# Gathers of a mixture-of-experts stage: four tiles a step for eight, and each gather waits for the last one

## What is computed

```python
edge_index = jnp.stack([src, dst])
x = x + _L0_gnn_ref(_layernorm(x), weight, bias, edge_index, edge_type_8)
x = x + _L0_ffn_ref(_layernorm(x)[None], gate_w, gate_b, w1, w2, w3)[0]

# _L0_gnn_ref: messages of 53125 edges of 8 types, summed over each target node
h_all = jnp.einsum('ni,roi->rno', node_repr, weight)
messages = jax.ops.segment_sum(h_all[edge_types, src], dst, num_segments=node_repr.shape[0])

# _L0_ffn_ref: the two best of 16 experts for each node, weighted
top_probs, top_idx = jax.lax.top_k(jax.nn.softmax(x @ gate_w + gate_b), 2)
hidden = jax.nn.silu(x @ w1[e]) * (x @ w2[e])      # hidden size 512
out = sum over the two experts of prob[e] * (hidden @ w3[e])
```

## Time and profile before

| | us |
|---|---|
| median of 3 runs | 969.27 |
| lowest, highest | 967.42, 971.19 |
| span of the profiled execution | 1205.6 |
| PE busy in it | 802.0 (67%) |
| POOL busy in it | 655.2 (54%) |
| DVE busy in it | 517.7 (43%) |
| mean granted clock of TensorE | 0.83 |

### The profile page before, as it was taken

How to read it: one execution, slowest core, us unless ns; L and a number is a source line. 1 busy time by engine, 2 the same in 40 slices (tenths; PEclk the granted TensorE clock), 3 DMA queues, 4 the chain that set the end, 5 groups by cost and what they waited for, 6 DMA issues and landing times.

```text
span 1205.6 us, 18175 instructions
## 1 busy us (share of the span) xinstructions
PE 802.0 (67%) x4527; PEld 664.8 (55%) x4528; DVE 517.7 (43%) x1480; ACT 262.8 (22%) x390; POOL 655.2 (54%) x614
## 2 busy tenths in 40 slices
PE   1355566666666677574666668657898889887761
PEld 1233355555555555463555556546787678776650
DVE  6753333333434344334333336786343334332327
ACT  5501111111111221111111111411232223221213
POOL 1366555555555666566555554045648583876442
PEclk9976687878878887797787788869898889997885
DMA  9434333333333322232222322336446554553325
GB/s 231 122 91 120 105 102 111 107 110 105 104 104 104 106 85 83 78 108 83 74 75 78 99 74 67 127 102 203 142 153 201 170 171 157 166 169 92 95 83 151
DMA packets 91426, 141.83 MB, mean 118 GB/s; under 512 B 13143, under 2 KB 65835, under 8 KB 91402
## 3 DMA queue, kind: packets, MB, share of 16 engines
q0 software_dynamic: 25680, 70.16, 20.2%
q1 hardware_dynamic: 48800, 56.26, 14.7%
q10 hardware_dynamic: 16922, 15.15, 3.9%
HBM read 108.59 MB, written 32.93 MB: 117 GB/s over the span
## 4 chain that ended last, share of the span: by engine, by line
PE 41%; another core or an unknown queue 18%; issue 17%; DVE 11%; DMA 4%; DVEq 4%; ACT 3%; ACTq 1%; SPq 1%; POOL 1%; POOLq 0%
PE ps L1426 16%; PE ps L1565 9%; PE ps L1547 6%; PE ps L1414 5%; DVE hot L981 2%; PE ps L1573 2%; PE ps L1456 2%; DVE store L999 2%; DMA acc<-in_x 1%; ACT store L699 1%; DVEq L999 1%; DVE stat L1016 1%; DVE ps L1348 1%; DVE acc L1012 1%
## 5 line engine op out<-in xcount | busy, mean ns | idle before, releaser
L541 POOL DMA_INDIRECT got<-x_tab,idx x425 | 403.5, 949 | 338.7 <-DVE idx L1001 188.6
L1414 PE MATMUL ps<-hot,got 125*128 125x256 f16 x1700 | 220.3, 289 | 65.3 <-issue 40.9
L999 DVE TENSOR_TENSOR store<-store,ps 128x512 f32 x150 | 103.0, 687 | 335.3 <-PE ps L1414 156.4
L1414 PEld LDWEIGHTS ps<-hot,got 125*128 125x128 f16 x1700 | 173.2, 103 | 110.8 <-issue 77.6
L1426 PE MATMUL ps<-part,store 128*128 128x256 f32 x800 | 222.4, 444 | 8.9 <-issue 8.4
L1426 PEld LDWEIGHTS ps<-part,store 128*128 128x128 f32 x800 | 180.1, 229 | 42.0 <-issue 11.3
L1565 PE MATMUL ps<-part,operands 128*128 x696 | 191.0, 426 | 6.9 <-DVE operands L1277 4.1
L1565 PEld LDWEIGHTS ps<-part,operands 128*128 128x128 f32 x696 | 137.6, 205 | 38.2 <-issue 8.8
L981 DVE TENSOR_SCALAR hot<-key_row,pass,drel 125x256 f16<-125x256 f16 x425 | 126.4, 354 | 74.0 <-issue 73.8
L1456 PE MATMUL ps<-gw_sb,x2T 128*125 128x16 f32 x100 | 23.1, 349 | 172.8 <-ACT x2T L691 105.2
L1547 PE MATMUL ps<-part,operands 128*128 x696 | 104.5, 303 | 30.8 <-DVE operands L1287 30.8
(11 more groups left out here) (229 smaller groups left out, 637.6 us busy)
## 6 DMA issues: line engine op xcount, KB each, us to landing
store<-in_L_ffn_w SPq DMA_DIRECT2D x48, 512.0 KB
y_tab<-ffn SPq DMA_DIRECT2D x9, 896.0 KB
y_tab<-ffn ACTq DMA_DIRECT2D x58, 128.0 KB
xs_tab<-x_sb SPq DMA_DIRECT2D x14, 512.0 KB
ffn<-xs_tab ACTq DMA_DIRECT2D x55, 128.0 KB
got<-x_tab,idx POOLq DMA_INDIRECT x425
acc<-in_x SPq DMA_DIRECT2D x5, 560.0 KB
x_tab<-got SPq DMA_DIRECT2D x5, 560.0 KB
```

The source lines that it names most:

```text
L541: nc.gpsimd.indirect_dma_start(got[:, c, :], None, x_tab, bass.IndirectOffsetOnAxis(ap=idx[:, c:c + 1], axis=0)).then_inc(gathered[c], 16)
L999: v.tensor_tensor(window, window, ps[:, WIN_BANK[g], :].rearrange("p (q n) -> p q n", n=WIN), ALU.add).then_inc(win_added, 1)
L1414: last = mm(ps[:, WIN_BANK[g], k * KEYS:(k + 1) * KEYS], got[0:CE, c, a * DIM + k * P:a * DIM + (k + 1) * P], hot[0:CE, g % HOT, c - c0, : ...
```

## The change

OCT, 8 tiles to a step, becomes QUAD, 4 tiles, and with it the half step that SP stores becomes two tiles (256 KB) for four. DVE's table quad_end counts in steps of four. The second part: inside a step, each gather from the second on waits until the one before has landed, and the 25 gathers of the first results do so too. The second results' gathers are as before.

```diff
-OCT = 8
-HALF_OCT = OCT // 2
+QUAD = 4
+HALF_QUAD = QUAD // 2
...
-                    sp.wait_ge(oct_got[n], (q + 1) * HALF_OCT * 16)
+                    sp.wait_ge(quad_got[n], (q + 1) * HALF_QUAD * 16)
...
-            def gather_oct(q):
+            def gather_quad(q):
                 pool.wait_ge(xs_stored, (q * 2 + 1) * 16)
                 pool.sem_inc(slot_free, 1)
-                nc.gpsimd.tensor_copy(oct_idx[:, :], token[:, bass.ds(q * OCT + DIRECT, OCT)]).then_inc(oct_ready, 1)
-                pool.wait_ge(oct_ready, q + 1)
+                nc.gpsimd.tensor_copy(quad_idx[:, :], token[:, bass.ds(q * QUAD + DIRECT, QUAD)]).then_inc(quad_ready, 1)
+                pool.wait_ge(quad_ready, q + 1)
                 pool.sem_inc(slot_free, 1)
-                for u in range(OCT):
+                for u in range(QUAD):
+                    if u:
+                        n = u - 1
+                        pool.wait_ge(quad_got[n // HALF_QUAD], q * HALF_QUAD * 16 + (n % HALF_QUAD + 1) * 16)
+                        pool.sem_inc(slot_free, 1)
                     nc.gpsimd.indirect_dma_start(
...
             for t in range(TILES):
                 if t % LOAD == 0:
                     wait_stored(0, t + LOAD - 1)
+                if t:
+                    pool.wait_ge(y_got[t - 1], 16)
                 nc.gpsimd.indirect_dma_start(
                     y1[:, t, :], None, y_tab,
                     bass.IndirectOffsetOnAxis(ap=pos2[:, 0, t:t + 1], axis=0)).then_inc(y_got[t], 16)
...
-                act.wait_ge(xs_stored, (j // HALF_OCT + 1) * 16)
+                act.wait_ge(xs_stored, (j // HALF_QUAD + 2 - DIRECT // HALF_QUAD) * 16)
```

More of the change, by code:

```diff
@@ L77 @@
 DIRECT = 4
-OCT = 8
-HALF_OCT = OCT // 2
-OCTS = -(-(SLOT_TILES + 2 - DIRECT) // OCT)
-XS_TILES = OCTS * OCT
+QUAD = 4
+HALF_QUAD = QUAD // 2
+QUADS = -(-(SLOT_TILES + 2 - DIRECT) // QUAD)
+XS_TILES = QUADS * QUAD
 ZT = 7
@@ L241, in build @@
         xs_ahead = sb("xs_ahead", [P, DIRECT - 2, DIM])
[L242 to L246, removed]
+        quad_idx = sb("quad_idx", [P, QUAD], I32)
+        quad_f = sb("quad_f", [1, EXPERTS])
+        quad_r = sb("quad_r", [1, EXPERTS], I32)
+        quad_end = sb("quad_end", [1, EXPERTS], I32)
+        xg = x_sb[:, 0:QUAD, :]
         low_hi = sb("low_hi", [TP, 2, TILES])
@@ L347, in build @@
         token_done = sem("token_done")
-        oct_ready = sem("oct_ready")
-        oct_got = [sem(f"oct_got{n}") for n in range(2)]
+        quad_ready = sem("quad_ready")
+        quad_got = [sem(f"quad_got{n}") for n in range(2)]
         xs_stored = sem("xs_stored")
@@ L490, in load_next, with store_quads @@
                 load_expert(e, k, sp.value_load(order[0:1, bass.ds(e, 1)], min_val=0, max_val=EXPERTS - 1))
-            def store_octs(e):
-                begin = sp.value_load(oct_end[0:1, bass.ds(e - 1, 1)], min_val=1, max_val=OCTS)
-                end = sp.value_load(oct_end[0:1, bass.ds(e, 1)], min_val=1, max_val=OCTS)
+            def store_quads(e):
+                begin = sp.value_load(quad_end[0:1, bass.ds(e - 1, 1)], min_val=1, max_val=QUADS)
+                end = sp.value_load(quad_end[0:1, bass.ds(e, 1)], min_val=1, max_val=QUADS)
                 with sp.If(begin < end):
                     with sp.Fori(begin, end) as q:
-                        store_oct(q)
+                        store_quad(q)
             sp.wait_ge(order_done, 1)
             load_next(2, 0)
-            store_oct(0)
+            store_quad(0)
             sp.wait_ge(owner_done, 4)
@@ L505, in _ @@
                     load_next(i * 2 + k + 1, 1 - k)
-                    store_octs(i * 2 + k)
+                    store_quads(i * 2 + k)
             load_next(EXPERTS - 1, 1)
-            store_octs(EXPERTS - 2)
-            store_octs(EXPERTS - 1)
+            store_quads(EXPERTS - 2)
+            store_quads(EXPERTS - 1)
             p0, p1 = SPREAD[0]
@@ L587, in _ @@
                     bass.IndirectOffsetOnAxis(ap=first_idx[:, u:u + 1], axis=0)).then_inc(xs_first[u], 16)
-            gather_oct(0)
+            gather_quad(0)
             pool.wait_ge(owner_done, 4)
@@ L591, in _ @@
                 for k in range(2):
-                    begin = pool.value_load(oct_end[0:1, bass.ds(i * 2 + k - 1, 1)], min_val=1, max_val=OCTS)
-                    end = pool.value_load(oct_end[0:1, bass.ds(i * 2 + k, 1)], min_val=1, max_val=OCTS)
+                    begin = pool.value_load(quad_end[0:1, bass.ds(i * 2 + k - 1, 1)], min_val=1, max_val=QUADS)
+                    end = pool.value_load(quad_end[0:1, bass.ds(i * 2 + k, 1)], min_val=1, max_val=QUADS)
                     used = pool.value_load(t_end[0:1, bass.ds(i * 2 + k - 2, 1)], min_val=1, max_val=SLOT_TILES)
@@ L1267, in oct_tables @@
                 v.tensor_copy(t_end[:, :], t_rank[:, :])
[L1268 to L1272, removed]
+                v.tensor_scalar(quad_f[:, EXPERTS - 1:], half_f[:, :], 2.0, float(QUAD - DIRECT), ALU.mult, ALU.add)
+                step(v.tensor_scalar(quad_f[:, 0:EXPERTS - 1], t_rank[:, 0:EXPERTS - 1], float(QUAD - DIRECT), float(QUAD), ALU.add, ALU.max))
+                step(v.tensor_copy(quad_r[:, :], quad_f[:, :]))
+                step(v.tensor_scalar(quad_end[:, :], quad_r[:, :], QUAD.bit_length() - 1, None, ALU.logical_shift_right))
+                v.memset(quad_end[:, 0:2], 1).then_inc(owner_done, 1)
             def low_xs(j):
@@ L1307, in _ @@
             split_first(0, (DOWN_PART,))
-            oct_tables()
+            quad_tables()
             expert_tile(0, 0, first=True)
```

16 lines of the change are left out of this document (8 added, 8 removed).

## The result

The changed kernel takes 1119.08 us (1117.14 to 1121.63, 4 runs) beside 968.35 us of the kernel before (4 runs): a ratio of 1.1554, 95% interval 1.1533 to 1.1576, 151 us more. I had said 1090, with a range of 1035 to 1125. In this document a median takes in all runs of a kernel, while a ratio and its interval leave out those over 1.5% above the kernel's fastest.

The account below looks back on a forecast made before the run. PE sets the expert stage's pace before; with the waits POOL becomes the bound. The changed kernel ends at 1270 against 1145 us on the profile's axis, +125; 969.3 + 125 = 1094, taken as 1090, range 1035 to 1125.

Parts of the forecast that it names:

- The 72 us of holdups: Expert stage of the old profile: 72 us of holdups, mostly PE products arriving late; a timed run has hardly room for them.
- The 10 us that I kept as real: Expert stage: some 10 us of the holdups taken as real, so the version without the others ends at about 1145 us.
- The period of a waiting gather: POOL's table steps and first results: a gather that waits for the last takes 3.3 us, where 1.25 stood.
- The weight load beside the first gather: Table steps: SP's 1.5 MB load holds the first gather up 2.9 us in 12 of 14 steps, 35 us.
- POOL's sum: Expert stage: table steps 166 us, load delays 35, 14 splits of 10.1 and 10 of waits; last split ends at 1153 us.
- The cover of the first results: After the last split: first results take 80 us, PE's last tiles only 39, so PE no longer covers them.
- The tail: Kernel end: 25 second gathers take 31 us, then landing 2.7, last sum 0.5 and last store 2.8, to 1270 us.
- the 4 us that I took off: Whole kernel: 1094 us lowered to 1090, since a timed run seemed, if anything, a little quicker per gather than the profile.
- Rival 1: Expert stage: holdups are in timed runs too and go with the bursts; up to 61 us back, likelier 1050 us; chance 0.14.
- Rival 2: Whole kernel faster: holdups real and gone, and the period short; with 2.0 us it would end at 947 us; chance 0.05.
- Rival 3: Waiting gathers: others' traffic slows landings, a period of 4.2 us adds 59, to 1150 us; chance 0.08.
- Rival 4: Expert stage: POOL's idle 69.5 us and PE's last tiles swallow the waits; no change, 969 us; chance 0.03.

Follow-up runs that it names:

- e7: The changed kernel again, unchanged, in a session where the kernel before took 1201.98 us: 1294.27 us, a ratio of 1.077.
- e6: The changed kernel with SP's load of the next weights put behind the stores of the step: 1266.52 us, 1.048 of the kernel before.
- e5: The changed kernel with two gathers under way, each waiting for the last but one: 1179.73 us, 0.982 of the kernel before.
- e1: The changed kernel without its new waits, steps of four tiles only: 1148.19 us, 0.983 of the kernel before.
- e4: The kernel before, steps of eight, with all the waits of the change: 1303.39 us, 1.088 of the kernel before.

## Why the prediction was right, point by point

- **The 72 us of holdups are not in a timed run.** Right for the runs compared: the stage begins at 627.37 us in the changed kernel's profile, where I had 625 for a graph stage with no pause. Wrong as a general statement: the holdups are in every profile of the disturbed sessions, and all times there are as long. The 1250 to 1290 us that I gave for the end of the changed kernel's profile did not come with the result (1119.9) but in e7 (1278.4). That the comparison met the undisturbed condition was partly luck; in the other one the change costs 92 us.
- **The 10 us that I kept as real** (1145 for the end of the version without holdups) were not there: its stage is 340 us by the estimate above, I had 350. That makes 10 us of the difference.
- **The period of a waiting gather**, 3.3 us "between the first two": the term that was mis-sized. Where the wait stands in the gather itself (line 621) it is 3.06 us on average, near my lower bound; in the steps, where a wait and a semaphore increment stand between, the shortest take 3.4 to 3.5 us, my upper bound, and the mean of the 28 later gaps is 3.88 us. One of these has the first step's weight load beside it (7.15 us); the other 27 average 3.76, probably since stores and loads of tiles are under way then. The chain of the changed kernel, at the end of the last step and among the first results, shows the parts, the landing (start to landing) and what follows it:

```profile
986.43 2.96 DMA x_sb<-x_tab,quad_idx
989.43 0.73 issue
...
1035.59 2.76 DMA x_sb<-y_tab,pos
```

 The first results were 6 us shorter than said (74 for 80), the steps' later gaps 16 us longer (28 x 0.58).
- **The weight load beside the first gather**: 2.9 us above 3.3, in 12 of 14 steps, made 81 us of first gaps; they sum to 84 (14 x 5.99). Eleven first gaps have the load, at 6.6 us on average, and three not, at 3.7; in the first step it falls on the second gap. So 12 gathers and 3 us each are right, and e6 shows the cause.
- **POOL's sum**: heads, splits and waits as said (9.7 us of waits for stores, forecast 10 in all waits of that kind; none for PE). From the first table step to the end of the last split 370.9 us, forecast 352.
- **The cover of the first results is gone**: right, PE ends 33 us before them.
- **The tail**: second results 30 us as said; from the last gather to the end 10.5 us where I had 6. The last sum of DVE starts 3.9 us after the last gather, and the last stores of the output take 6 us, not the 2.8 us that the old trace showed behind a chain bound by DVE. 4 us more.
- The sum: 125 + 10 + 19 - 6 + 4 = 152 us, the 492.5 less 340 of the stage. The misses add up nearly all one way, which puts the result near the upper end of the range. And the 4 us that I took off for a timed run "a little quicker per gather" should not have been: gathers go out at the same 1.25 us.
- **Rival 1** ("up to 61 us come back") is what happens in the disturbed condition, with nearly that size: 62 us of stage. The holdups are real there. Even so the waits cost more than the holdups: the change is 92 us slower there, where this rival with a period of 3.3 us had 64. Rival 2 fails on the period, as said. Rival 3 (other traffic slows the landings) is true in part: the later gaps lie between the forecast and its 4.2 us. Rival 4 has no support: POOL's idle time was used up entirely.

By the Trainium skill, DMA: Bandwidth & Descriptors, rules for kernel authors, one issues a DMA early, computes, and waits for it late, so that the fixed cost overlaps. The trace agrees: of the 3.03 us between two first results 2.03 are idle waiting, and with one more gather under way POOL waits 56 us for landings in the steps where it waited 151 (e5, e7).

## What to carry to other kernels

A wait for a landing on an in-order queue costs the landing (2.8 us here, for 128 KB) plus 0.3 to 0.7 us until the next one starts, and everything behind it in the queue pays: count what the queue has free (69.5 us here) against the number of waits times that, before asking what the wait may help. If a limit on transfers under way is wanted, two or three cost a fraction of one: 46 and 20 us here, against 152. And when a profile's span is 20% off the timed runs, build the floor of each stage from its rows and ask which of them fits in the timed total, before a term of the sum is taken from a wait that may not be there.

## What the runs showed of the hardware

- The same kernel takes 968 or 1168 to 1202 us by session. In the disturbed sessions, DVE and ACT wait up to 17.6 us (e1) for something that the trace doesn't name while the matmuls before it stand in the records as done, often beside bursts of indirect gathers on POOL. With one or two gathers under way, this all but vanished from the expert stage (a gauge of 0 in e4, e6 and e7, of 1.7 us in e5). Both disturbed sessions ran on chip 13 and the later undisturbed one on chip 4, so the chip may be what differs; three sessions don't show it. Whether number or spacing of the gathers matters is open: the two runs meant for that met an undisturbed session.
- The granted clock of TensorE goes with it but is not enough to explain it. For the kernel before, means over the span are 0.886 to 0.896 in session 4 and 0.820 to 0.848 in sessions 2 and 3; for the changed kernel 0.842 to 0.849 in session 1 and 0.799 to 0.807 in session 3. In the graph stage of the changed kernel (clock 0.86 and 0.81) PE is busy 459 and 492 us, 33 us more, while the stage takes 155 us more. Whether the lower clock is a cause or follows from PE's idle time is open.
- Beside 1.5 MB of weights sent by SP (0.03 us earlier in the lines above), the first gather of a step is followed by the next after 6.6 us on average, without them after 3.7. With the load behind the step the mean of all first gaps is 3.79 us (e6).
